# The opening of a one-core vision tower: zero products first, row 0 in two parts, part of row 1 on VectorE, group 4 by halves

## The reference, cut to what matters

```python
lu, ru, ld, rd = _shifts(x)                       # four copies of x, shifted by 4 pixels in both directions
concat = concatenate((x, lu, ru, ld, rd), axis=1) # 5 shifts x 2 channels
mean, var = concat.mean(per image), concat.var(per image)
normed = (concat - mean) * rsqrt(var + 1e-7) * gamma + beta
y = conv(normed, W, stride 8)                     # 13 x 13 = 169 tokens of 128 channels, 64 images
h = [cls_tok, y + b]
q, k, v = layernorm(h) @ Wq.T, @ Wk.T, @ Wv.T
for t in tokens:                                  # one state of 128 x 128 over all images
    S = S + 0.01 * v_t.T @ k_t;  out_t = q_t @ S.T
h = h + out;  h = h + ffn(layernorm(h))
```

## Time and profile before

| what | value |
|---|---|
| median of 3 runs | 217.61 us (217.36 to 217.68) |
| the profiled execution | 217.46 us |
| its span | 215.6 us |
| PE busy | 196.3 us, 91% |
| DVE, ACT, POOL busy | 71%, 59%, 72% |
| chain that ended last | PE 52%, POOL 15%, DMA 10%, DVE 8% |
| image loads, of that chain | 10% |

### The profile page before, as it was taken

One profiled execution on the slowest core, in us unless ns is written; L12 is line 12 of the kernel. 1 busy time (PEld: TensorE's weight loads), 2 busy tenths in 40 slices (PEclk: granted clock), 3 DMA queues, 4 the chain that ended last, 5 costly groups with the idle time before them and its releaser, 6 DMA issues.

```text
span 215.6 us, 5028 instructions
## 1 busy us (share of the span) xinstructions
PE 196.3 (91%) x1548; PEld 166.9 (77%) x1548; DVE 152.3 (71%) x758; ACT 127.7 (59%) x306; POOL 154.5 (72%) x129
## 2 busy tenths in 40 slices
PE   0699999999999999999999999999999999999720
PEld 0488897886888889788888888899888888888610
DVE  3639694684486675678687597687687687699892
ACT  4215777884443375475756565665665574577982
POOL 1069908899990999969999949938999541455671
PEclk9999999999999999999999999999999999999975
DMA  5999992745022006153053432022012012100356
GB/s 140 388 420 422 422 413 112 217 185 181 0 58 111 2 3 194 30 175 88 3 153 109 125 93 49 5 50 49 11 41 52 16 36 52 28 22 5 80 118 152
DMA packets 17216, 25.90 MB, mean 120 GB/s; under 512 B 1719, under 2 KB 13693, under 8 KB 17062
## 3 DMA queue, kind: packets, MB, share of 16 engines
q1 hardware_dynamic: 16486, 25.41, 36.5%
q10 hardware_dynamic: 704, 0.17, 0.4%
HBM read 19.65 MB, written 5.92 MB: 119 GB/s over the span
## 4 chain that ended last, share of the span: by engine, by line
PE 52%; POOL 15%; DMA 10%; DVE 8%; issue 7%; SPq 4%; ACT 2%; POOLq 0%; DVEq 0%; ACTq 0%
PE conv L575 25%; DMA images<-x_rows 10%; PE vr_ps L623 10%; POOL scaled L469 7%; PE first_ps L633 6%; PE outs L650 6%; POOL rstd L1337 3%; PE turn L608 3%; POOL g_low L1327 2%; DVE state L1007 2%; DVE state L999 2%; SPq L488 1%; PE conv L583 1%; DVE images L1028 1%; POOL rstd L1353 1%
## 5 line engine op out<-in xcount | busy, mean ns | idle before, releaser
L575 PE MATMUL conv<-scaled,wt 128*128 128x256 f32 (+3 forms) x432 | 111.7, 375 | 7.3 <-DMA wt<-weight 6.9
L469 POOL TENSOR_TENSOR scaled<-rows,gam 128x832 f32<-128x832 f32 (+1 forms) x54 | 84.7, 1588 | 17.6 <-DMA rows<-x_windows 17.3
L575 PEld LDWEIGHTS conv<-scaled,wt 128*128 128x128 f32 x432 | 71.7, 193 | 15.3 <-DMA wt<-weight 6.9
L817 ACT ACTIVATE values<-vr_ps,rstd 128x256 f32<-128x256 f32 x76 | 36.0, 473 | 62.8 <-PE vr_ps L623 50.1
L1337 POOL TENSOR_TENSOR rstd<-var,powers 128x8 f32<-128x8 f32 (+2 forms) x20 | 30.3, 1517 | 27.0 <-DVE var L1019 26.9
L999 DVE TENSOR_TENSOR state<-first_ps,state 128x128 f32<-128x128 f32 x76 | 22.1, 291 | 27.6 <-PE first_ps L633 22.2
L825 ACT ACTIVATE images<-images,ln_shift,ln_gain 128x128 f32<-128x128 f32 x80 | 37.3, 489 | 1.5 <-DVE ln_shift L1076 0.7
L623 PE MATMUL vr_ps<-w_high,g_low 128*128 128x256 f32 x77 | 30.8, 400 | 0.8 <-ACT values L817 0.8
L1327 POOL TENSOR_TENSOR g_low<-g_t,g_high 128x512 fp32r<-128x512 f32 x21 | 26.8, 1274 | 4.6 <-ACT g_high L804 4.6
L988 DVE BATCH_NORM_STATS2 ln_stats<-images 128x6 f32<-128x128 f32 x85 | 23.6, 284 | 4.8 <-ACT images L811 4.7
L1007 DVE TENSOR_TENSOR state<-second_ps,state 128x128 f32<-128x128 f32 x76 | 21.5, 282 | 2.1
(11 more groups left out here) (201 smaller groups left out, 273.5 us busy)
## 6 DMA issues: line engine op xcount, KB each, us to landing
rows<-x_windows SPq DMA_DIRECT2D x12, 864.0 KB, 4.8
out<-images SPq DMA_DIRECT2D x40, 128.0 KB, 2.4
images<-x_rows SPq DMA_DIRECT2D x4, 832.0 KB, 14.9
images<-x_rows SPq DMA_DIRECT2D x1, 1040.0 KB, 15.9
images<-x_rows SPq DMA_DIRECT2D x1, 624.0 KB, 20.7
rows<-x_windows SPq DMA_DIRECT2D x1, 448.0 KB, 6.1
gam<-gamma SPq DMA_DIRECT2D x1, 422.5 KB, 6.8
bet<-beta SPq DMA_DIRECT2D x1, 422.5 KB, 9.0
```

Of the source, the lines that this page charges most:

```text
L469: return eng.tensor_tensor(scaled[:, s, at + skip:at + N], window[:, skip:N], gains.unsqueeze(2).to_broadcast([P, N - skip, B]), ALU.mult)
L575: last = pe.matmul(conv_ps[g % 2][:, at:at + n * B], held, scaled[:, s, a % RING:a % RING + n], start=first, stop=(g < EARLY and s >= TOP ...
L817: act.activation(values[:, t % VALUE_SLOTS].rearrange("p a e -> p (a e)"), vr_bank(t)[:, 0:2 * E], ACT.Identity, scale=rho_of(t)).then_inc ...
```

## The change

- TensorE begins with three products of zeros (128x512) into a bank that nothing reads yet, and puts a fourth between shift 0 and shift 1 of group 0.
- VectorE scales row 0 in two parts, first the eight tokens of group 0 for all four shifts, then the other five. Then it scales three tokens of row 1 for all five shifts (a new semaphore, `scaled_second`); GpSimd scales the other ten.
- The gamma table comes first, waiting for gamma alone; then shifts 0 and 1 of group 1; then the beta table. Shifts 2 to 4 of group 1 stay where group 1 was.
- VectorE makes the low parts of the tables after the first image chunk and not after the second.
- Group 4 is issued by halves: the first half of each shift, the second half of each. Five pieces stand ahead of the sums, four behind, one behind the product of `scale_cols`; then the first two pieces of group 5. Nothing of group 4 is left behind `early`.
- `FIRST` begins with 4 instead of 2, and step -8 leaves out the two pieces issued before it.

```diff
-FIRST = (2, 2, 1, 1, 1, 1, 1, 1)
+AHEAD = 2
+FIRST = (4, 2, 1, 1, 1, 1, 1, 1)
...
+SECOND = 2 * TOKENS
...
             if a // N == 0:
-                eng.wait_ge(scaled_first, s + 1)
+                eng.wait_ge(scaled_first, s + 1 if a < TOKENS else TOP + 1 + s + 1)
...
+            elif 0 < last and a + n <= SECOND:
+                eng.wait_ge(scaled_second, s + 1)
             elif last > 0:
                 eng.wait_ge(scaled_rows, pool_scales(last, s))
...
-        def scale_shift(eng, r, s):
+        def scale_shift(eng, r, s, first=0, stop=N):
...
+                if r == ROW_SLOTS:
+                    sp.wait_ge(scaled_second, SHIFTS)
...
-            sp.wait_ge(scaled_first, TOP + 1)
+            sp.wait_ge(scaled_first, 2 * (TOP + 1))
             load_row(3)
...
+            def conv_fifth(a, z):
+                items = conv_items(EARLY - 1)
+                for item in (items[0::2] + items[1::2])[a:z]:
+                    conv(item)
...
-                share = [i for i, st in enumerate(ITEM_STEPS) if st == t]
+                share = [i for i, st in enumerate(ITEM_STEPS) if st == t and i >= AHEAD]
...
+            def zero_products(count):
+                for _ in range(count):
+                    pe.matmul(vr_ps[:, 0:PER_GROUP * E], zeros[:], zeros[:].unsqueeze(1).to_broadcast([P, PER_GROUP, E]),
+                              start=True, stop=True, skip_group_check=True)
+
+            pe.wait_ge(zeros_ready, 1)
+            zero_products(3)
             pe.wait_ge(weight_in, 16)
-            conv_shifts(0, 0, SHIFTS)
-            pe.wait_ge(gamma_in, 16)
-            pe.wait_ge(beta_in, 16)
-            for kind, table in enumerate((bet, gam)):
+            conv_shifts(0, 0, 1)
+            zero_products(1)
+            conv_shifts(0, 1, SHIFTS)
+            def table_columns(kind, table):
...
+            pe.wait_ge(gamma_in, 16)
+            table_columns(1, gam)
+            conv_shifts(1, 0, 2)
+            pe.wait_ge(beta_in, 16)
+            table_columns(0, bet).then_inc(columns_done, 1)
...
-            conv_shifts(1, 0, SHIFTS)
+            conv_shifts(1, 2, SHIFTS)
...
             conv_shifts(3, 0, SHIFTS)
+            conv_fifth(0, 5)
             pe.wait_ge(sums_ready, 2)
...
-            conv_shifts(EARLY - 1, 0, 2)
+            conv_fifth(5, 9)
             pe.wait_ge(scale_cols_ready, 1)
...
-            conv_shifts(EARLY - 1, 2, 4)
+            conv_fifth(9, 10)
+            for item in LATE_ITEMS[0:AHEAD]:
+                conv(item)
...
-            conv_shifts(EARLY - 1, 4, SHIFTS)
...
-                scale_shift(dve, 0, s).then_inc(scaled_first, 1)
+                scale_shift(dve, 0, s, 0, TOKENS).then_inc(scaled_first, 1)
+            for s in range(TOP + 1):
+                scale_shift(dve, 0, s, TOKENS).then_inc(scaled_first, 1)
+            dve.wait_ge(gamma_in, 16)
+            dve.wait_ge(row_in[1], 16)
+            for s in range(SHIFTS):
+                scale_shift(dve, 1, s, 0, SECOND - N).then_inc(scaled_second, 1)
...
-                scale_shift(pool, r, s).then_inc(scaled_rows, 2 if (r, s) == (N - 1, BOTTOM) else 1)
+                scale_shift(pool, r, s, SECOND - N if r == 1 else 0).then_inc(scaled_rows, 2 if (r, s) == (N - 1, BOTTOM) else 1)
```

More of the change, by code:

```diff
@@ L319, in tower @@
         scaled_first = sem("scaled_first")
+        scaled_second = sem("scaled_second")
         scaled_rows = sem("scaled_rows")
@@ L463, in scale_shift @@
             window = rows[:, r % ROW_SLOTS, 0:N] if s == 0 else rows[:, offsets, right:right + N]
-            skip = 1 if r * N == CORNER else 0
-            gains = gam_first[:, s] if r == 0 else gam[:, s, r * N + skip:r * N + N]
+            skip = 1 if r * N == CORNER else first
+            gains = gam_first[:, s, skip:stop] if r == 0 else gam[:, s, r * N + skip:r * N + stop]
             if (r, s) == (N - 1, BOTTOM):
@@ L468, in scale_shift @@
             at = r % 2 * N
-            return eng.tensor_tensor(scaled[:, s, at + skip:at + N], window[:, skip:N],
-                                     gains.unsqueeze(2).to_broadcast([P, N - skip, B]), ALU.mult)
+            return eng.tensor_tensor(scaled[:, s, at + skip:at + stop], window[:, skip:stop],
+                                     gains.unsqueeze(2).to_broadcast([P, stop - skip, B]), ALU.mult)
         block = ctx.enter_context(nc.Block())
@@ L713, in _ @@
                                      stop=(i == SHIFTS - 1), skip_group_check=True)
-            last.then_inc(columns_done, 1)
+                return last
+            pe.wait_ge(gamma_in, 16)
[3 more added lines that the diff above has]
+            table_columns(0, bet).then_inc(columns_done, 1)
             pe.wait_ge(small_in, 16)
@@ L1260, in _ @@
                         last_stats = dve.bn_stats(stats[:, 2 * j:2 * j + 2].rearrange("p a b -> p (a b)"), part)
+                if i == 0:
+                    for blk, ps in enumerate((turn_ps, second_ps)):
+                        m = P if blk == 0 else PATCHES - P
+                        dve.wait_ge(table_high_ready, blk + 1)
+                        dve.tensor_tensor(term_parts[0:m, blk, :, 1], ps[0:m, 0:2 * E].rearrange("p (k e) -> p k e", e=E),
+                                          term_parts[0:m, blk, :, 0], ALU.subtract).then_inc(table_low_ready, 1)
                 if i == 1:
@@ L1265, in _ @@
                                              ALU.subtract).then_inc(w_low_ready, 1)
-                    for blk, ps in enumerate((turn_ps, second_ps)):
-                        m = P if blk == 0 else PATCHES - P
-                        dve.wait_ge(table_high_ready, blk + 1)
-                        dve.tensor_tensor(term_parts[0:m, blk, :, 1], ps[0:m, 0:2 * E].rearrange("p (k e) -> p k e", e=E),
-                                          term_parts[0:m, blk, :, 0], ALU.subtract).then_inc(table_low_ready, 1)
             last_stats.then_inc(stats_step, 1)
```

## The result

| | before | the change |
|---|---|---|
| median of 4 runs | 217.63 us (217.36 to 217.68) | 219.96 us (219.65 to 220.92) |
| profiled execution, its span | 217.46, 215.6 us | 220.92, 219.1 us |
| mean granted clock in it | 0.982 | 0.964 |

The ratio is 1.0114, with a 95% interval of 1.0096 to 1.0132: **slower by 2.3 us**. That is inside the range and on the wrong side of the forecast. The profiled execution is the longest of the four, so its delays are larger than the median's.

A forecast was written before the change was run, and what follows sets the result against it. TensorE, busy 91% of the span and all of the long loop, was taken as the bound. Terms -1.72 (four products), -0.1 and -0.2 (holes), +0.15 (late sums) gave -1.87: 215.7 us on the median, range 215.1 to 221.7.

The forecast's parts named there:

- VectorE's win at 47.41: Old trace, loop: VectorE went first although GpSimd's next product had been issued; evidence against the engines taking turns.
- The lead: TensorE's opening: four more convolution products done before `early`, 1.72 us less behind it, plus loop holes shrinking 0.1 and 0.2.
- holes: TensorE's waits for ScalarE's `values` in the loop, 0.37 and 0.24 us; forecast to give 0.1 and 0.2.
- the one at 51.41: TensorE's 0.37 us wait for `values` in the loop; forecast to shrink by about 0.1.
- the one at 91.87: TensorE's 0.24 us wait for `values`, behind GpSimd's run from 69.85; forecast to give 0.2 us.
- The rival of a lead that does not last: Loop: only 0.86 us before the wait at 51.41 survive, as GpSimd and ScalarE then pace; 216.7 us, chance 0.12.
- the rival of zeros that do not raise the clock: Opening: group 0 stays slow, ends at 14.05, sums 2.1 late, gain eaten; 217.4 us, chance 0.07.
- The turns rival: Row 1: VectorE and GpSimd scalings alternate, delaying `small` 4.1 us and the centred weights; 221.4 us (219 to 223), chance 0.36.
- a stand of 2.0 us: TensorE's wait before the centred weights; the length from which the case of alternating scalings decides.
- The fall: TensorE's clock drops in a stand of 4.5 us; 4 to 6 us at half rate add 1.5 to 3, from 219.4 to 221.4.

The follow-up runs named there:

- the stand filled: The change plus four more products of zeros where TensorE stands before the centred weights: 218.56 us, ratio 1.0047.
- the kernel in which GpSimd waits: The change, but GpSimd starts its part of row 1 only when VectorE's five products of row 1 are done: 215.22 us, ratio 0.9898; again 215.15.
- its old group 4: The change with group 4 and the late products in the order of the kernel before: 220.23 us, ratio 1.0124.

## Why the prediction was wrong

**The step that failed** is "VectorE now takes the three tokens that group 1 needs, 5 x 0.27 us, from the same moment, to 14.2, still before 14.80". They took to 18.57. The row that I had of such a meeting showed each engine waiting for a whole instruction of the other; from VectorE's win at 47.41 and its overlapping records I took it that VectorE would pass all five. It passes one. So `w_stats` started 3.7 us late (18.50 for 14.80), the weights' products 3.4 us (20.32 for 16.90), and `early` 5.69 us, of which 2.36 are the clock's fall (43.25 against 40.89 with the stand filled). A product queued ahead does not keep its engine in possession: after each GpSimd product VectorE had one, after each VectorE product GpSimd had one, in every run where both queued.

**Steps that held**, shown by the kernel in which GpSimd waits: group 0 at full rate to 11.9 (11.5), weights' products at 16.68 (16.5), group 2 at 21.95 (22.0), sums at 33.24 (33.3), `early` at 37.33 (37.5). It took 215.2 us for a forecast of 215.7. The lead was priced at 1.72 for four products and 0.3 for holes, 2.0; it is 2.2. Of the holes, the one at 51.41 did not shrink (0.38 at 50.27), the one at 91.87, 0.24 us, is gone; where the other 0.2 us of the lead come from no run shows. The rival of a lead that does not last falls: 2.2 us last in every kernel with the halves. So does the rival of zeros that do not raise the clock.

**The turns rival** had the mechanism and most places: fifth product ended 18.57 (18.9), centred weights' products at 20.32 (20.6), decided beyond a stand of 2.0 us (3.49). Its price was too high. Without the clock's fall it said 219.4, and the filled stand measured 218.56: `early` is 3.33 late there and not 3.9, and the lead 0.2 larger. The fall was priced at 2.0 and costs 1.4 of the median (219.96 against 218.56); in the profiled execution, where it lasts for nearly all of the seven microseconds from 19, it costs 2.3 (220.92 against 218.59).

**The zeros** were not priced apart in the sum; the rival without their effect, at 217.4 for a forecast of 215.7, gives them 1.7 us. They pay 0.5 to 0.7 us where TensorE has work to go on with, nothing on the kernel before, and in the change they cost 1.5. The rival had group 0 end at 14.05 and the sums come 2.1 us late; without zeros it ended at 13.58 and 12.77, and the sums were reached at 34.50 and 33.69, 1.3 and 0.5 us later than with them.

The Trainium skill ("SBUF — State Buffer", section "SBUF: two separate sides") calls the pair of ports an exclusive lock that goes to the engine that starts first, for the whole instruction, and the other fully blocks. The runs agree for a single meeting (0.36 us becomes 1.41). Where both engines keep a queue, the runs show strict alternation, one instruction each.

Not tried: whether the alternation holds for other pairs of operations than products of two SBUF tensors, and what makes the clock fall in some executions of a kernel and not in others after the same stand.

## What to carry to other kernels

Small elementwise products of two SBUF tensors on VectorE are not small beside a stream of long GpSimd ones: count each as one GpSimd instruction long, and look at what is queued behind them on VectorE. Either let VectorE go first with one wait on GpSimd, if GpSimd's end has slack, or cut GpSimd's instructions. A speedup upstream of a fixed arrival only makes the stand longer, and a longer stand of TensorE can cost the clock: give it work that is due anyway, or leave the speedup out.

## What the runs showed of the hardware

- VectorE and GpSimd products of two SBUF tensors alternate, one instruction each, in all six profiled executions where both queued: VectorE's 128x192 takes 0.36 us alone and 1.41 held by GpSimd's 128x640, 0.87 held by its 128x320. GpSimd's own go from 1.26 to 1.37: the short one costs the long one a tenth of a microsecond, the long one costs the short one 1.05 us. VectorE's batch statistics, which read one SBUF tensor, are not held: 128x384 take 0.54 to 0.57 us beside GpSimd's scaling (before, 17 to 21 us) and 0.55 without it (27.6 to 29.5 us).
- Products of zeros raise TensorE's clock: with three of 128x512 from 1.03 us, the first convolution at 6.9 runs at the full rate (four records in 1.13 us, 2.07 without zeros). The Trainium skill ("TensorE: Matmul & The Clock Gate", section "What's actually happening") has activity as what releases the clock; the trace agrees, and operands that are all zeros do not keep it from rising.
- Behind the same stand the clock can fall or not, execution by execution. Where TensorE stood 3.49 us it fell in both kernels profiled (the change and its old group 4). Where it stood 2.28, 2.02 and 1.7 us, some executions took 1.2 us and more longer than the middle of the others: six of ten, two of ten, and three of twenty in two kernels. The two profiled ones among these show the half rate; for the others only their lower mean clock speaks (0.966 to 0.978, against 0.978 to 0.986).
- The fall need not come in the stand: it came in it at 19 us in the change, and 0.7 to 1.4 us behind its end, while TensorE was at work again, in the three other profiled executions that have one.
